# Weighted sums of a group's first two key chunks issued as one visit, in an attention and mixture-of-experts kernel

## What is computed

```
x = x + attention(layernorm(x), ctx, ctx, k_length)    # 8 heads of 32 channels, 512 queries, 512 keys
x = x + moe(layernorm(x))                              # 4096 rows, 8 experts, top 2, 512 -> 2048 -> 512

# attention, per head: q, k, v are (d=32, 512)
attn = softmax(s * einsum('dq,dk->qk', q, k));  out = einsum('qk,dk->dq', attn, v)
```

## Time and profile before

| | |
|---|---|
| median of three runs | 2185.14 us |
| the profiled execution | 2179.5 us, span 2177.8 us |
| attention steps 0 to 31 | 0 to about 615 us |
| tail | 615 to about 655 us |
| router's last work and dispatch | to 677 us |
| expert layer | 677 us to the end |

### The profile page before, as it was taken

How to read it: one execution, slowest core, us unless ns; L and a number is a source line. 1 busy time by engine, 2 the same in 40 slices (tenths; PEclk the granted TensorE clock), 3 DMA queues, 4 the chain that set the end, 5 groups by cost and what they waited for, 6 DMA issues and landing times. The chain is left out here.

```text
span 2177.8 us, 27085 instructions
## 1 busy us (share of the span) xinstructions
PE 2117.0 (97%) x10179; PEld 1518.8 (70%) x10179; DVE 1008.1 (46%) x1908; ACT 712.9 (33%) x1216; POOL 470.4 (22%) x593
## 2 busy tenths in 40 slices
PE   3999999999999999999999999999999999999997
PEld 1445454455547888878888887888888788888776
DVE  5677878878765434234324423423432342343211
ACT  1666666666652222113212212311311231132110
POOL 3334444343422111110301201031030102101101
PEclk9999999999999999999999999999999999999999
DMA  9876767776635435212613612422441252241101
GB/s 147 160 165 157 181 157 188 168 187 162 146 114 161 115 70 132 58 22 85 131 20 78 150 26 58 125 50 43 114 98 25 56 134 52 48 125 31 16 6 20
DMA packets 183895, 216.61 MB, mean 99 GB/s; under 512 B 39731, under 2 KB 111419, under 8 KB 183740
## 3 DMA queue, kind: packets, MB, share of 16 engines
q1 hardware_dynamic: 154128, 173.21, 34.1%
q0 software_dynamic: 22240, 37.92, 9.1%
q10 hardware_dynamic: 7372, 3.42, 0.7%
HBM read 113.93 MB, written 68.29 MB: 84 GB/s over the span
## 5 line engine op out<-in xcount | busy, mean ns | idle before, releaser
L1590 DVE SCALAR_TENSOR_TENSOR hlo<-ps_h,hhi 128x512 fp32r<-128x512 f32 x256 | 177.0, 692 | 928.4 <-ACT hhi L1467 928.4
L1467 ACT ACTIVATE hhi<-ps_h 128x512 fp32r<-128x512 f32 x256 | 152.9, 597 | 1123.4 <-PE ps_h L1731 1123.4
L1729 PE MATMUL ps_h<-xhi,w1hi 128*128 128x512 f32 x1024 | 404.9, 395 | 2.5 <-PEq L1316 1.3
L1748 PE MATMUL ps_y<-w2hi,hhi 128*128 128x512 f32 x1024 | 404.7, 395 | 0.7 <-DVE hlo L1590 0.7
L1749 PE MATMUL ps_y<-w2lo,hhi 128*128 128x512 f32 x1024 | 403.0, 394 | 1.0 <-issue 1.0
L1750 PE MATMUL ps_y<-w2hi,hlo 128*128 128x512 f32 x1024 | 403.7, 394 | 0.0
L1731 PE MATMUL ps_h<-xhi,w1lo 128*128 128x512 f32 x1024 | 403.6, 394 | 0.0
L1730 PE MATMUL ps_h<-xlo,w1hi 128*128 128x512 f32 x1024 | 403.0, 394 | 0.0
L678 DVE TENSOR_REDUCE nmax<-ps_s 128x1 f32<-128x512 f32 x512 | 335.7, 681 | 128.5 <-PE ps_s L1086 124.6
L460 ACT ACTIVATE probs<-ps_t 128x512 f32<-128x512 f32 x504 | 273.0, 604 | 183.1 <-PE ps_t L1037 145.8
L1729 PEld LDWEIGHTS ps_h<-xhi,w1hi 128*128 128x128 f32 x1024 | 192.3, 188 | 48.5 <-issue 3.9
(11 more groups left out here) (202 smaller groups left out, 2007.2 us busy)
## 6 DMA issues: line engine op xcount, KB each, us to landing
raw<-in_L_ffn_w SPq DMA_DIRECT2D x128, 512.0 KB, 4.9
qst<-qhi SPq DMA_DIRECT2D x64, 256.0 KB, 5.8
xin<-dispatched SPq DMA_DIRECT2D x60, 256.0 KB, 5.8
kst<-khi SPq DMA_DIRECT2D x52, 256.0 KB, 6.4
xt<-in_x SPq DMA_DIRECT2D x32, 256.0 KB, 3.1
ct<-in_ctx SPq DMA_DIRECT2D x32, 256.0 KB, 4.5
qst<-qlo SPq DMA_DIRECT2D x32, 256.0 KB, 6.8
xres<-in_x SPq DMA_DIRECT2D x32, 256.0 KB, 4.7
```

Of the source, the lines that this page charges most:

```text
L1467: nc.scalar.activation(hhi[k % 2][:], ps_h[k % 3][:], ACT.Relu).then_inc(hhi_ready, 1)
L1590: nc.vector.scalar_tensor_tensor(hlo[k % 2][:], ps_h[k % 3][:], 0.0, hhi[k % 2][:].bitcast(F32), ALU.max, ALU.subtract).then_inc(h_ready, 1)
L1729: nc.tensor.matmul(to, w1hi[:, c, fs], xhi[n % 2][:, c, :], start=(c == 0), stop=False)
L1748: nc.tensor.matmul(ps_y[b][:], hhi[k % 2][:, bs], w2hi[:, f, :], start=(f == 0), stop=False)
```

## The change

In steps 2 to 31 and in the tail, the visit for chunk 0 of a group moves from the end of chunk 1's turned scores to just before the visit for chunk 1, in chunk 2. No instruction is added or removed.

```
@@ -1113,8 +1113,11 @@
                     if c == 0 and live(s - 3):
                         weighted(s - 3, NC4 - 1)
-                    if c > 0 and live(s - 2):
-                        weighted(s - 2, c - 1)
+                    if c == 2 and live(s - 2):
+                        weighted(s - 2, 0)
+                        weighted(s - 2, 1)
+                    if c == 3 and live(s - 2):
+                        weighted(s - 2, 2)
@@ -1127,7 +1130,13 @@
                     turned_logits(g, c, 1)
                     if g == G - 2 and c == 0:
                         shares(G - 4)
-                    weighted(g if c else g - 1, (c - 1) % NC4)
+                    if c == 0:
+                        weighted(g - 1, 3)
+                    if c == 2:
+                        weighted(g, 0)
+                        weighted(g, 1)
+                    if c == 3:
+                        weighted(g, 2)
                     if c == 0:
                         row_turned(g - 3)
```

## The result

Six runs of the changed kernel gave 2189.82 to 2196.33 us, median **2193.94 us**. The medians differ by 11.8 us. The measured ratio is **1.0049, 95% interval 1.0035 to 1.0062**, which is 10.7 us. The profiled execution took 2193.59 us (span 2191.8 us), 14.1 us more than that of before.

The account below looks back on a forecast made before the run. PE was taken to set the pace, with DVE often just in time. Loop +9.9 us and tail -3 us gave +6.9 us on the median of 2185.1 us: 2192 us, range 2187 to 2198 (chance 0.55), 8 in 10 within 2179 to 2201.

Parts of the forecast that it names:

- the two waits: Chunk 2: s(2,0) held by DVE's multiplication in odd steps, 0.43 us lost; V held by ACT in even steps, 0.52 us.
- Rival 1: Loop chunk 2: PE hardly waits, so saving 0.28 us a step by merging wins; 2174.5 us, chance 0.14.
- rival 2: Loop: waits of 0.3 to 0.45 us a step cancel the merging's saving; 2181 to 2189 us, chance 0.21.
- rival 3: Loop and tail: the delay reaches chunk 3, 0.65 us a step, and the tail's clock falls; 2205 us, chance 0.10.
- Odd step, +0.33 forecast: Loop, 14 odd steps 5 to 31: s(3,0) comes 0.33 us later, the merging's saving included; 4.6 us in all.
- even step, +0.41: Loop, 13 even steps 6 to 30: s(3,0) comes 0.41 us later, the merging's saving included; 5.3 us in all.
- a bank is free some 0.05 us after its reader's end: Chunk 2: PE can reuse a bank about 0.05 us after DVE or ACT finishes reading it.
- the walk: Step-by-step timing of PE, DVE, ACT and banks through chunk 2, from t(1,3) to s(3,0), for odd and even steps.
- the double visit: End of chunk 2: the visits for chunks 0 and 1 back to back on PE, lasting 3.61 us.
- The tail, -3 forecast: Tail: waits for ACT's probabilities and DVE's reciprocal disappear, 1.5 us for each of two groups less some tenths; -3 us.
- the clock's part: Tail, 640 to 655 us: left at zero; 1.7 us gained if PE keeps 2.4 GHz, 1.8 to 3.5 lost otherwise.
- The claim that the rest of a step is unchanged: Loop: outside t(1,3) to s(3,0), a step keeps its order and time, so only that stretch changes.

Follow-up runs that it names:

- run 3: Changed kernel with ACT's copy of the keys moved from the end of chunk 1 to between its copies of X and V in chunk 2; 2182.15 us, ratio 0.9995.
- run 4: Changed kernel with DVE's multiplication of the share directly behind the maximum of s(1,1), small router operations behind s(1,2); 2188.44 us, ratio 1.0025.
- run 2: Kernel before with only the loop part of the change, the tail as before; 2196.73 us, ratio 1.0064.
- run 8: The changed kernel measured again, unaltered; 2197.38 us, ratio 1.0056.
- run 1: Kernel before with only the tail part of the change, the loop as before; 2179.46 us, ratio 0.9983.
- run 11: Tail part of the change alone, loop as before, measured on another occasion; 2180.78 us, ratio 0.9982.
- run 5: Changed kernel with both moves: ACT's keys copy later, DVE's multiplication of the share and router operations reordered; 2205.96 us, ratio 1.0091.
- run 10: Run 5 with POOL's residual ahead of its keys subtraction, and DVE's reciprocal, cast and subtraction for shares behind the scaled queries; 2185.08 us, ratio 1.0000.
- run 12: Run 10 with DVE's router operations moved one place later in every second step; 2177.50 us, ratio 0.9976.
- run 6: Run 5 with the loop's visits separate as before and the tail as changed; 2240.43 us, ratio 1.0242.

## Why the prediction was right, and where its sizes were off

The forecast was 2192 us with a loss of 6.9 us; measured are 2193.94 us and, by the ratio, 10.7 us (7.6 to 13.5). The direction and the two waits are right. That the time is met within 2 us is in part luck: the base of the forecast, 2185.14 us, was the median of three runs and lies 3.0 us above the median of six, and this made up for most of the loss that the sum lacked.

- **Which engine holds PE.** Right in both kinds of step: DVE's multiplication before s(2,0) (+0.67 forecast, +0.68 measured), ACT's second probability before V in the even step (+2.4 and +2.56). Runs 3 and 4 show both causes by moving them. Rival 1 (the saving wins) fails on the stretch, 7.46 and 7.63 us instead of under 7.0; rival 2 (they cancel) on the ratio's interval, whose lower end is 1.0035; rival 3 on chunk 3, which is as before.
- **Odd step, +0.33 forecast, +0.42 measured; even step, +0.41 and +0.48.** The term that was too small is "a bank is free some 0.05 us after its reader's end", used for V. In the even step ACT's t(2,0) ends near 328.81 + 0.59 = 329.40 (a single one takes 0.59 to 0.60), and V starts at 329.57, 0.17 us later. In the odd step it ends at 309.40 + 0.59 = 309.99, just where the walk had put it, and V starts at 310.17, 0.18 us later. On the other side the double visit lasts 315.24 - 311.67 = 3.57 us, not 3.61. In the sum this counts for little: 27 equal steps would give 12.1 us, but six of the steps lose less (above), so the waits are 10.6 us, against +9.9 forecast.
- **The odd step's V is bounded by ACT as well.** In the forecast's walk both waits stand in the odd step, but I spoke of DVE's as its cause. Run 4 took that one away and the stretch stayed at 7.45: the two are in a row, and only the last decides.
- **The tail, -3 forecast, -5.0 in the profile.** The waits and the gap before ps_l are gone as forecast. Against run 2's old tail, at the same clock, this is -3.3. The other 1.7 us are the clock's part, which I had named and set to zero; as run 2 has it with the old tail too, it is not shown to be the change's.
- **Missing: the clock and late shares in the loop.** I weighed the clock in the tail alone, and took all else in a step as unchanged. The two falls, the two late shares and the waits at the end of step 30 are behind the 6.6 us that the sum lacks (above). A fall costs about 1.4 us. The changed kernel's first profile has 1 from 100 to 600 us, the repeat 6, the loop-only one 5. What makes one wait end in a fall and the next not is open. It is not the sum of waits: the changed kernel waits 10.6 us in all and has one, run 8 waits 10.0 us and has six. Runs 1 and 11 have one and two, each behind a late share. Run 4's 5 us under the changed kernel fit fewer falls: over all its executions the mean granted clock is 0.995 to 0.997, against 0.992 to 0.996 in the changed kernel and 0.990 to 0.993 in run 8. But this was not isolated.

The claim that the rest of a step is unchanged holds for its time, but it hid that DVE's comparison (line 746) had grown from 528 to 843 ns and the addition behind it (line 751) from 176 to 585 ns, under the double visit, where nobody waited for them.

## What to carry to other kernels

When a visit that covers two other engines is moved, walk each bank from its reader's end; two waits in a row must both be removed before anything is gained, and moving the work that causes them moves its followers on a third engine too. After a reordering, look for small vector operations that have grown: if each ends with a GpSimd operation beside it, order the two engines' work so that they don't meet. But first ask whether somebody waits for them: in run 3 they had grown as much as in run 5 and nothing was lost. Try such a change first where the waits are (here the tail), alone.

## What the runs showed of the hardware

**DVE behind POOL.** A small DVE operation that starts while POOL is in a 1.28 us operation of two SBUF inputs ends 0.02 to 0.06 us after POOL's. Six rows above show it (runs 5, 10 and 12); in the kernel before, hot with 305.72 + 0.53 = 306.25 beside POOL's 304.92 + 1.27 = 306.19; and in the changed kernel 310.97 + 1.28 = 312.25 beside 310.91 + 1.29 = 312.20. From 60 to 655 us in all 14 profiles, 407 such operations start at least 0.05 us behind one of POOL's, and 403 of them end 0.02 to 0.06 us after it (one 0.09). In the other four, hot starts 0.05 or 0.06 us behind POOL's residual and keeps its 0.18 us (one 0.19), and it is POOL's operation that takes longer, 1.38 us instead of 1.28. Affected are operations with two SBUF inputs (pr, hot, picked, before, the subtraction) and the cast from SBUF to SBUF. The row maxima, which read PSUM, keep 0.68 us beside the same POOL operations. In the Trainium skill, "SBUF — State Buffer", section "SBUF: two separate sides", the port pair that VectorE shares with GpSimd is an exclusive lock: whoever starts first has it for the whole instruction, "the other fully blocks". By that rule the end times should be as they are, and the trace agrees, with 0.05 us between the two ends. The page's rule would also have foretold from POOL's new place that these operations grow in run 5; I had not looked at POOL, since none of its instructions had moved in the text of the program.

**The clock.** PE falls to the 1.2 GHz level for some 3 us within a stream that is 98% busy. In the rows of run 2 above, s(2,0) had waited 0.19 us, and the share's multiplication on PE 0.41 us for its DMA 1.8 us earlier; from 230.59 on the rows are at the lower level, and the visit at 234.06 is at 2.4 GHz again. In that run the falls come at 230.6, 309.1, 387.6, 465.8 and 544.3 us, 78 to 79 us or four steps apart, in steps that look alike. Run 8 has the same distance between its first five, from 191.1 to 505.4 us. In run 5 they come 41 us apart where they follow each other, in run 6 in places 21 us.
